# The third slot tile's high and low parts as one 128-column stationary operand, with the halves added on VectorE

## What is computed

```
logits = xf @ gate_w.T                       # 2048 tokens, 16 experts
top_vals, sel = top_k(sigmoid(logits), 2);  weights = top_vals / (sum + 1e-6)
slot = expert * capacity + rank in expert    # capacity = 320; later tokens are dropped
padded = zeros.at[slot].set(tokens)          # [16, 320, 256]
h   = gelu(einsum('ecd,edf->ecf', padded, w1))      # w1 [16, 256, 512]
out = einsum('ecf,efd->ecd', h, w2)                 # w2 [16, 512, 256]
x  += tanh(g_ffn) * (sum over a token's two slots of weight * out)
```

## Time and profile before

| | us |
|---|---|
| median of 3 runs | 358.88 (356.75 to 359.57) |
| the profiled execution, its own time | 359.79 |
| its span, first to last instruction | 358.0 |
| TensorE busy in the span | 318.3 |
| VectorE / ScalarE / GpSimd busy | 222.7 / 204.8 / 208.3 |
| mean granted TensorE clock, share of full speed | 0.956 |

### The profile page before, as it was taken

How to read it: one execution, slowest core, us unless ns; L and a number is a source line. 1 busy time by engine, 2 the same in 40 slices (tenths; PEclk the granted TensorE clock), 3 DMA queues, 4 the chain that set the end, 5 groups by cost and what they waited for, 6 DMA issues and landing times. The chain is left out here.

```text
span 358.0 us, 6349 instructions
## 1 busy us (share of the span) xinstructions
PE 318.3 (89%) x2147; PEld 276.1 (77%) x2147; DVE 222.7 (62%) x523; ACT 204.8 (57%) x569; POOL 208.3 (58%) x266
## 2 busy tenths in 40 slices
PE   7998998899999999997667999999999999999700
PEld 2456777799888999976523899999999999999600
DVE  0688887467887877776670376666666666666000
ACT  1465868488888778773350366666556666654200
POOL 7044338644677878765683105666676667676660
PEclk9999999899999999998969999999999999999955
DMA  5999998000021111111223847777877887844440
GB/s 171 261 308 298 191 190 135 15 17 16 19 71 62 45 46 46 45 52 54 74 90 108 274 156 190 187 181 186 218 191 193 193 204 193 210 62 43 48 51 8
DMA packets 39354, 45.67 MB, mean 128 GB/s; under 512 B 4165, under 2 KB 33370, under 8 KB 39322
## 3 DMA queue, kind: packets, MB, share of 16 engines
q1 hardware_dynamic: 31858, 35.77, 36.5%
q0 software_dynamic: 7424, 9.48, 15.1%
q10 hardware_dynamic: 40, 0.02, 0.0%
HBM read 28.01 MB, written 17.24 MB: 126 GB/s over the span
## 5 line engine op out<-in xcount | busy, mean ns | idle before, releaser
L504 POOL DMA_INDIRECT out_dram<-wqT,rows_to x48 | 82.6, 1721 | 58.8 <-DMA out_dram<-wqT,rows_to 31.7
L1118 PE MATMUL ps_scores<-value_t,score_t 128*128 128x320 f32 x384 | 59.2, 310 | 0.0
L1118 PEld LDWEIGHTS ps_scores<-value_t,score_t 128*128 128x128 f32 x384 | 56.5, 188 | 0.4 <-DVE value_t L881 0.3
L1031 PE MATMUL ps_scores<-score_t,xn 128*128 128x512 f32 x192 | 54.7, 430 | 0.0
L1065 PE MATMUL ps_out<-value_t,pT 128*128 128x256 f32 x384 | 53.1, 290 | 0.1
L1065 PEld LDWEIGHTS ps_out<-value_t,pT 128*128 128x128 f32 x384 | 48.0, 193 | 0.8 <-DVE x L781 0.6
L888 DVE TENSOR_TENSOR score_t<-raw,score_t 128x1024 fp32r<-128x1024 f32 x16 | 19.6, 1224 | 40.6 <-ACT score_t L629 40.6
L1134 PE MATMUL ps_out<-score_t,value_t 128*128 128x256 f32 x336 | 43.9, 287 | 0.0
L1031 PEld LDWEIGHTS ps_scores<-score_t,xn 128*128 128x128 f32 x192 | 37.1, 193 | 7.1
L1134 PEld LDWEIGHTS ps_out<-score_t,value_t 128*128 128x128 f32 x336 | 41.0, 191 | 0.9
L452 POOL TENSOR_TENSOR probs<-probs,norm 128x1024 f32<-128x1024 f32 x16 | 30.5, 1904 | 16.1 <-DVE norm L822 16.1
(11 more groups left out here) (160 smaller groups left out, 593.4 us busy)
## 6 DMA issues: line engine op xcount, KB each, us to landing
raw<-in_L_ffn_w_dram SPq DMA_DIRECT2D x32, 512.0 KB
padded<-xg SPq DMA_DIRECT2D x2, 2064.0 KB, 28.5
xg<-padded SPq DMA_DIRECT2D x16, 258.0 KB
out_dram<-x SPq DMA_DIRECT2D x16, 128.0 KB, 1.7
padded<-xg SPq DMA_DIRECT2D x1, 1032.0 KB, 30.3
xg<-padded SPq DMA_DIRECT2D x16, 64.5 KB
wq_sb<-in_L_xattn_Wq_dram SPq DMA_DIRECT2D x1, 1024.0 KB, 8.5
wo_sb<-in_L_xattn_Wo_dram SPq DMA_DIRECT2D x1, 1024.0 KB, 5.7
```

The lines of the kernel that those rows point to most:

```text
L504: pool.indirect_dma_start(out, bass.IndirectOffsetOnAxis(ap=rows_to[0:SLOTS[k], e, k:k + 1], axis=0), y[0:SLOTS[k], j, k], None, compute_o ...
L1031: op = pe.matmul(dst, xn[:, j, a, c], mv, start=False, stop=last)
L1118: op = pe.matmul(ps_scores[:, f, 0:CAPACITY], w1_hl(p, a)[:, c, f * P:(f + 1) * P], x_hl(p, b)[:, c], start=c == 0 and (a, b) == PARTS[0], ...
```

## The change

- h's layout: for each chunk f the 320 high and the 320 low columns now lie side by side, and for the third slot tile the 64 low columns are written right behind the 64 high ones. So `h_third` is one stationary operand of 128 columns: high in columns 0 to 63, low in 64 to 127.
- TensorE: the third tile is 8 matmuls instead of 12. For each f one matmul of `h_third` with w2's high part, whose result fills 128 partitions of `ps_misc`, and one of the high part with w2's low part, into partitions 0 to 63. Between tile 1 and tile 3 it waits for `y_last` of the expert before.
- ScalarE: for the third tile it now moves partitions 64 to 127 of `ps_misc`, scaled by the slot weight, to the new tile `y_low` (64x256).
- VectorE: at the end of its step one `scalar_tensor_tensor` computes partitions 0 to 63 of `ps_misc` times slot weight plus `y_low` into y and raises `y_last`. The low part of h is two subtractions instead of one (2x256 and 2x64 elements) in each half.
- SyncE: a third DMA per fetch brings token and weight columns (8 bytes each) of the 64 rows to partitions 64 to 127 too, and `fetched` counts 48.
- GpSimd: the first scatter waits for tiles 0 and 1 only, the third for `y_last`.

```diff
+        y_low = sb("y_low", [P - SLOTS[2], DIM])
...
+        def h_both(p):
+            n = 2 * FC * CAPACITY
+            return value_t[:, p * n:(p + 1) * n].rearrange("p (c s) -> p c s", c=FC)
+
+        def h_high_of(p):
+            return h_both(p)[:, :, 0:CAPACITY]
+
+        def h_low_of(p):
+            return h_both(p)[:, :, CAPACITY + SLOTS[2]:]
+
+        def h_third(p):
+            return h_both(p)[:, :, 2 * P:2 * P + 2 * SLOTS[2]]
...
                     sp.dma_start(xg[0:SLOTS[2], e % 2, 2], padded[at + 2 * P:at + CAPACITY, :]).then_inc(fetched[e % 2], 16)
+                    sp.dma_start(xg[SLOTS[2]:, e % 2, 2, TOKEN:], padded[at + 2 * P:at + CAPACITY, TOKEN:]).then_inc(fetched[e % 2], 16)
...
                 for k in range(SLOT_TILES):
-                    if near_end(e) or k == 0:
-                        pool.wait_ge(y_ready, SLOT_TILES * e + k + 1 if near_end(e) else SLOT_TILES * (e + 1))
+                    if k == SLOT_TILES - 1:
+                        pool.wait_ge(y_last, e + 1)
+                    elif near_end(e) or k == 0:
+                        pool.wait_ge(y_ready, 2 * e + k + 1 if near_end(e) else 2 * e + 2)
...
                         act.wait_ge(y_made, SLOT_TILES * e + (2 if k == 0 and not near_end(e) else k + 1))
+                        if k == SLOT_TILES - 1:
+                            wait(act, y_last, e)
+                            act.activation(y_low[:, :], ps_misc[SLOTS[k]:, 0:DIM], ACT.Copy,
+                                           scale=slot_w[SLOTS[k]:, e, k:k + 1]).then_inc(y_lowered, 1)
+                        else:
...
-                        dve.tensor_tensor(lo, h_full[:, 2 * h:2 * h + 2], hi.bitcast(F32), ALU.subtract).then_inc(h_low, 1)
+                        dve.tensor_tensor(h_low_of(p)[:, fs], h_full[:, 2 * h:2 * h + 2][:, :, 0:n], h_high_of(p)[:, fs, 0:n].bitcast(F32), ALU.subtract)
+                        dve.tensor_tensor(h_third(p)[:, fs, SLOTS[2]:], h_full[:, 2 * h:2 * h + 2][:, :, n:], h_high_of(p)[:, fs, n:].bitcast(F32),
+                                          ALU.subtract).then_inc(h_low, 1)
                 if e >= 0:
                     rows_low(e + 2, j)
+
+                if exists(e, EXPERTS):
+                    n = SLOTS[2]
+                    wait(dve, added[j], SLOT_TILES * 16 * i)
+                    dve.wait_ge(marked, e + 1)
+                    dve.wait_ge(y_lowered, e + 1)
+                    dve.scalar_tensor_tensor(y[0:n, j, 2], y_bank(e, 2), slot_w[0:n, e, 2:3], y_low[:, :], ALU.mult, ALU.add
+                                             ).then_inc(y_last, 1)
...
+                    wait(pe, y_last, e)
+                    at = P * (SLOT_TILES - 1)
+
+                    def third(f, low):
+
+                        if low:
+                            return pe.matmul(y_bank(e, 2), h_high_of(j)[:, f, at:], w2_hl(j, 1)[:, f], start=False, stop=False)
+                        return pe.matmul(ps_misc[:, 0:DIM], h_third(j)[:, f], w2_hl(j, 0)[:, f], start=f == 0, stop=f == FC - 1)
+
+                    for f in range(FC - 1):
+                        third(f, False)
+                        third(f, True)
+                    third(FC - 1, True)
+                    third(FC - 1, False).then_inc(y_made, 1)
```

More of the change, by code:

```diff
@@ L194, in w2_hl @@
             return score_t[:, (4 * p + 2 + k) * 1024:(4 * p + 3 + k) * 1024].rearrange("p (c d) -> p c d", c=FC)
-        def h_hl(p, k):
-            n = FC * CAPACITY
-            return value_t[:, (2 * p + k) * n:(2 * p + k + 1) * n].rearrange("p (c s) -> p c s", c=FC)
+        def h_both(p):
[7 more added lines that the diff above has]
+            return h_both(p)[:, :, 2 * P:2 * P + 2 * SLOTS[2]]
         def x_hl(p, k):
@@ L257, in build @@
         h_made, h_act, h_high, h_low = sem("h_made"), sem("h_act"), sem("h_high"), sem("h_low")
-        y_made, y_ready = sem("y_made"), sem("y_ready")
+        y_made, y_ready, y_lowered, y_last = sem("y_made"), sem("y_ready"), sem("y_lowered"), sem("y_last")
         JOBS = [("ctx", 0)] + [("kr", n) for n in range(2)]
@@ L489, in mark @@
                 if exists(e, EXPERTS):
-                    pool.wait_ge(fetched[e % 2], 32 * (e // 2 + 1))
+                    pool.wait_ge(fetched[e % 2], 48 * (e // 2 + 1))
                     done.mark(pool.tensor_scalar(rows_to[:, e], xg[:, e % 2, :, TOKEN], 0.0, None, ALU.add))
@@ L657, in expert @@
                         act.wait_ge(y_made, SLOT_TILES * e + (2 if k == 0 and not near_end(e) else k + 1))
-                        act.activation(y[0:SLOTS[k], j, k], y_bank(e, k), ACT.Copy,
-                                       scale=slot_w[0:SLOTS[k], e, k:k + 1]).then_inc(y_ready, 1)
+                        if k == SLOT_TILES - 1:
[3 more added lines that the diff above has]
+                        else:
+                            act.activation(y[0:SLOTS[k], j, k], y_bank(e, k), ACT.Copy,
+                                           scale=slot_w[0:SLOTS[k], e, k:k + 1]).then_inc(y_ready, 1)
             expert_steps(expert)
@@ L896, in expert @@
                     for h in range(2):
-                        hi, lo = (h_hl(p, k)[:, 2 * h:2 * h + 2] for k in range(2))
+                        fs, n = slice(2 * h, 2 * h + 2), 2 * P
                         dve.wait_ge(h_act, 2 * t + h + 1)
                         wait(dve, y_made, SLOT_TILES * (t - 1))
-                        dve.tensor_copy(hi, h_full[:, 2 * h:2 * h + 2]).then_inc(h_high, 1)
+                        dve.tensor_copy(h_high_of(p)[:, fs], h_full[:, 2 * h:2 * h + 2]).then_inc(h_high, 1)
                         dve.wait_ge(h_high, 2 * t + h + 1)
-                        dve.tensor_tensor(lo, h_full[:, 2 * h:2 * h + 2], hi.bitcast(F32), ALU.subtract).then_inc(h_low, 1)
+                        dve.tensor_tensor(h_low_of(p)[:, fs], h_full[:, 2 * h:2 * h + 2][:, :, 0:n], h_high_of(p)[:, fs, 0:n].bitcast(F32), ALU.subtract)
+                        dve.tensor_tensor(h_third(p)[:, fs, SLOTS[2]:], h_full[:, 2 * h:2 * h + 2][:, :, n:], h_high_of(p)[:, fs, n:].bitcast(F32),
+                                          ALU.subtract).then_inc(h_low, 1)
                 if e >= 0:
                     rows_low(e + 2, j)
+                if exists(e, EXPERTS):
[5 more added lines that the diff above has]
+                                             ).then_inc(y_last, 1)
             expert_steps(expert)
@@ L1097, in turn @@
                     wait(pe, x_low, t)
-                    pe.wait_ge(fetched[j], 32 * (i + 2))
+                    pe.wait_ge(fetched[j], 48 * (i + 2))
                     for k in range(SLOT_TILES):
@@ L1128, in second_product @@
                     pe.wait_ge(h_low, 2 * e + 2)
-                    for k in range(SLOT_TILES):
-                        if k == (2 if near_end(e) else 0):
-                            wait(pe, y_ready, SLOT_TILES * e)
+                    for k in range(SLOT_TILES - 1):
+                        if k == 0 and not near_end(e):
+                            wait(pe, y_ready, 2 * e)
                         for f in range(FC):
                             for a, b in PARTS:
-                                op = pe.matmul(y_bank(e, k), h_hl(j, a)[:, f, k * P:k * P + SLOTS[k]], w2_hl(j, b)[:, f],
+                                op = pe.matmul(y_bank(e, k), (h_low_of(j) if a else h_high_of(j))[:, f, k * P:(k + 1) * P], w2_hl(j, b)[:, f],
                                                start=f == 0 and (a, b) == PARTS[0], stop=f == FC - 1 and (a, b) == PARTS[-1])
                         op.then_inc(y_made, 1)
+                    wait(pe, y_last, e)
[9 more added lines that the diff above has]
+                    third(FC - 1, False).then_inc(y_made, 1)
             def expert(e, j, i):
```

## The result

In a joint series on the chip the changed kernel took 0.9876 of the time of the kernel before (95% interval 0.9839 to 0.9912): 4.45 us of 358.88, where 4.6 was forecast. This ratio compares only executions within 1.5% of their kernel's fastest, which are 6 of the changed kernel's 21 and 16 of the 21 of before, while the medians over all 21 are 360.45 for the changed kernel and 359.31 for the kernel before. The changed kernel's executions spread from 351.9 to 367.9, those of before from 356.8 to 366.2, and the profiled execution of the changed kernel is a late one, with a span of 365.9. A second series, with 12 runs of the changed kernel, gave 0.9944 (0.9889 to 1.0), and medians over all runs of 361.24 against 359.93. So the forecast size was met in one series and less than half of it in the other, and by the medians over all runs nothing was gained. What eats the gain shows in the trace.

The account below looks back on a forecast made before the run. TensorE's work was taken to set the pace at 8.66 us per expert, the end hanging on GpSimd's scatters. 6.0 - 0.5 - 0.6 - 0.3 = 4.6 off the median of 358.88 gave 354.3, range 352.0 to 358.6.

Parts of the forecast that it names:

- The forecast's own case: GpSimd's first scatter issues keep their place in VectorE's pattern, cycles of 8.2, gain 4.6; chance 0.49.
- TensorE, 0.43 per expert: Third tile on TensorE: 1.37 becomes 0.94, period 8.23, 6.0 us saved by expert 13.
- VectorE's sum, 0.475, hidden: New 64x256 sum on VectorE takes 0.475 and fits in the idle time ahead of its next subtraction.
- Split, 0.18 per half: Low part of h on VectorE: a second subtraction instruction costs 0.18 in each half, from 0 to 0.2.
- The third tile's wait: TensorE's wait for y_last costs nothing; B(e) is when TensorE leaves the second product of expert e.
- Expert 13's held issue, 0.3: GpSimd's first scatter issue of expert 13 meets VectorE's last copy and subtraction: 0.3 lost, 0 to 1.0.
- Third fetch DMA, 0.5 at the start: SyncE's extra DMA delays expert 0's fetch, on the path to TensorE's start: 0.5 lost, 0 to 1.0.
- For experts 2 to 15 fetches run two steps ahead, cost zero.: SyncE's third fetch DMA, 0.48 to issue, costs nothing after the first experts since fetches run two steps ahead.
- Rival 1: GpSimd's first scatter issue falls into a later slot of VectorE's pattern: price 1.35, gain 3.25, 355.6; chance 0.20.
- Rival 2: GpSimd finishes its scatter issues unhindered by VectorE: gain 5.5 to 6.0, 353.1; chance 0.09.
- Rival 3: GpSimd's scatter loop is the bound if holds stay as long: gain 0.5 to 1, 358.1; chance 0.12.
- Rival 4: Denser traffic and 64 tiny packets per expert lengthen the scatters' landing; at 3.7 slower, 362.5; chance 0.10.

Follow-up runs that it names:

- experiment 4: Changed kernel without the third fetch DMA, ScalarE moving the low half without slot weight: 1.0004 of the kernel before, median 360.88.
- Experiment 10: Kernel before with 8 instead of 12 matmuls in the third tile and slot targets and weights copied one expert earlier: 0.9836, median 353.37.
- Experiment 12: Changed kernel with slot targets and weights copied one expert earlier, run once more: 0.9842 of the kernel before, median 353.23.
- experiment 5: Changed kernel with slot targets and weights copied one expert earlier, first run: 0.9818 of the kernel before, median over all runs 357.04.
- experiment 9: Changed kernel with copies one expert earlier and the fetch between the two weight loads: 0.9862 of the kernel before, median 353.81.
- experiment 2: Kernel before with 8 instead of 12 matmuls in the third tile, nothing added: 1.0009 of the kernel before.
- experiment 11: Changed kernel with copies one expert earlier and no third fetch DMA, low half without slot weight: 0.9831 of the kernel before, median 353.32.
- experiment 3: Kernel before plus the third fetch DMA of 64 x 8 bytes per expert: 0.9982 of the kernel before.
- experiment 8: Kernel before with the w2 load held so that both weight loads of a step leave together: 0.9946, median over all runs 361.82.

## Why the forecast held, and where its reasons did not

The number was right: 4.6 forecast, 4.45 measured, inside the range, and the direction too. That it fits to 0.15 is in part luck. The second series gave 2.0 us, the medians over all runs gave nothing, and the two traces of the changed kernel fail the forecast's own test. That test was expert 13's first scatter, which was to start at least 3.6 us earlier. Counted from the first transpose it started 131.35 into the stage before, and 135.4 and 135.1 in the changed kernel's traces, 4 us later. The forecast's own case is seen in the trace of experiment 4, the changed kernel without the third fetch: the first issues of experts 1 to 7 end at B + 5.5, and expert 13's first scatter starts at 126.6, 4.7 earlier than before. Step by step:

- *TensorE, 0.43 per expert.* Measured 0.44 (1.37 to 0.93; period 8.66 to 8.22 in every trace of the changed kernel where nothing waits). Right.
- *VectorE's sum, 0.475, hidden.* Measured 0.48 in the place named. Right. *Split, 0.18 per half:* too much. The two parts take 0.69 and 0.28 but overlap; from one half's subtraction to the next copy it was 0.74 before and is 0.81 now, 0.07 more.
- *The third tile's wait.* The prediction has it come 6.9 after B(e-1); it comes 7.3 after (282.49 to 289.78). Nothing hangs on that.
- *The additions on the whole.* Experiment 10 against 12: 353.37 and 353.23, no difference; by stage number 0.4. Right that they are small.
- *Expert 13's held issue, 0.3:* nothing. It takes 1.6 to 1.8 in the traces of experiments 4, 5, 9 and 12, and took 1.75 before.
- *Third fetch DMA, 0.5 at the start:* too much. From the first fetch issue to the first transpose it took 3.2 to 3.8 in the seven traces of kernels with it (mean 3.42), and 3.1 to 3.5 in the seven without (mean 3.19): 0.2 by the means.
- *"For experts 2 to 15 fetches run two steps ahead, cost zero."* This is the step that failed. The fetch has time to spare, but SyncE's queue doesn't: it waits for GpSimd's copies, and the weight loads stand behind it. I had the idle time of the data and not the order of the queue. What the runs showed in its place: with TensorE at 8.2 the loop's cycle was 9.00, 9.00 and 8.84 where the fetch waits for fresh copies (the changed kernel twice, experiment 2), with one execution that kept up at 8.29 (experiment 4), and 8.19 to 8.21 in all four traces where only the copies are made an expert earlier (experiments 5, 10, 11 and 12). The forecast's case, GpSimd keeping its slot, describes the changed kernel's trace only for its first cycles: expert 2's first issue ends at 238.92, B(2) + 5.75 as forecast, experts 3 and 5 likewise. Then one landing of 3.8 throws it out.
- *Rival 1, the later slot.* Experiment 12 lives in it: its first issues end between B + 6.9 and B + 7.1 from expert 2 to 10, where 7.1 was forecast. By my terms the stage number would then fall by 6.0 - 0.6 - 0.3 - 1.35 = 3.75; it fell by 4.4. The slot cost some 0.6 less than its 1.35, and was never the danger. In experiment 9 the first issues of experts 3 to 7 keep the forecast's slot (B + 5.76), and the stage number is the same 156.5.
- *Rival 2, no hindrance.* Not seen, though the mean issue of experts 1 to 13 went from 1.76 to 1.60 in experiment 12.
- *Rivals 3 and 4.* Cycles of 9.0 did come, at landings about 3.1 on average, with TensorE waiting at the end. Rival 3's condition came true in these traces: the issues stayed as long as before (1.73 and 1.75 on average against 1.76), and they make half of the distance to experiment 12. As a bound of its own it fails, since with the early copies the issues fall to 1.59 to 1.63. Rival 4 had the landings right and their cause wrong: the small packets are not needed (experiments 2 and 3), and what goes with the longest landings is traffic that leaves in one burst. "It hardly follows the load" was read from the earlier trace rows, where loads and scatters kept their distance; it holds only for that.
- *Held issues.* The row of 2.72 shows the hold on GpSimd's copies as well. The Trainium skill (SBUF — State Buffer, Who interferes with whom) says of a tensor_tensor with both inputs in SBUF that it contends with GpSimd's reads. By that rule this row is to be expected, and the trace agrees: 0.23 alone, 2.72 beside two such subtractions and a copy.

So the 0.9876 is best read as the worth of the change where the loop stays in step, though no trace shows such an execution of the changed kernel itself; by the medians over all its executions nothing was left of it. With the copies one expert earlier the ratio is 0.9842, 0.9818 and, with the other order as well, 0.9862. Experiment 12's median is 5.6 below that of before, its stage number 4.4; where the other 1.2 come from is not shown. Not settled is what decides in a given execution whether GpSimd falls out of step, and the long landings at a greater distance have no cause named.

Why the stages ahead vary is open too, but in the longest three it goes with TensorE's clock. The page's clock line, changed kernel and before:

```profile
PEclk9959999899999999998969999999999999999555
...
PEclk9999999899999999998969999999999999999955
```

The third slice, 18 to 27 us, has about half the clock in the changed kernel's trace, which is the lower level of 1.2 GHz. Over 17.0 to 27.5 us the granted clock is 0.51 to 0.54 in three traces (the changed kernel, experiments 4 and 11) and 1.00 in the eleven others. The three reach the stage at 199.8 to 201.5, the others at 193.7 to 197.1. What lowers it is not shown. So 4 to 5 us of the span of 365.9 are not the scatters' doing, and the stage number is the fairer comparison of these traces.

## What to carry to other kernels

Before trusting a saving on the busiest engine, work out the next loop's cycle and its spread, not its mean; here it had 0.2 us of room per turn (8.0 against 8.22). Look at each in-order queue for a DMA that waits on an engine off the critical path, and ask what stands behind it: a late helper can turn evenly spaced transfers into a burst, and the burst makes the helper later. Decoupling such a wait cost nothing measurable where it wasn't needed (0.9993) and carried the saving where it was (0.9836 against 1.0009). And look at all executions: this change took the lowest time from 356.8 to 351.9 and the median from 359.3 to 360.5.

## What was not expected of the hardware

- A scatter-add whose last issue starts under 2.5 us after a 512 KB load's took 3.8 to 5.9 us to land (6 cases), against 2.9 on average otherwise (134 cases, 8 of them 3.8 or more).
- A GpSimd copy of 128x3 elements, 0.23 us alone, took up to 3.01 beside VectorE's subtractions from SBUF (experiment 8), and a scatter issue of 1.57 took 2.67 there (changed kernel).
- A DMA of 64 pieces of 8 bytes for each of 16 experts changed the time by less than could be measured (0.9982, interval 0.9946 to 1.0019).
